# Second mixer: per-image products as 32x32 tiles of TensorE, layer norms applied by ScalarE, row loop written out

## The reference, cut to what matters

```python
x = x + _L1_conv_ref(_ln_c(x), ...)            # _ln_c: layer norm over the 96 channels, eps 1e-6

zxbcdt = xf @ W_in                             # z (192), xBC (224), dt (12)
dt = softplus(dt + dt_bias)
xBC = silu(conv3x3_depthwise(xBC) + b_conv)    # x_inner 192, B_state 16, C_state 16
Y_diag = einsum('bclhn,bcshn,bhcls,bcshp->bclhp', Cm, Bm, L, X)
states = einsum('bclhn,bhcl,bclhp->bchpn', Bm, decay_states, X)
Y_off  = einsum('bclhn,bchpn,bhcl->bclhp', Cm, states, state_decay_out)
y = Y_diag + Y_off + x_inner * D_param
y = layernorm(y, eps=1e-5) * gamma + beta      # over 192
y = (y * silu(z)) @ W_out
```

## Time and profile before

| | |
|---|---|
| median of 3 runs | 2666.05 us (2660.29 to 2674.77) |
| profiled execution | 2666.47 us, its span 2664.7 us |
| busy in the span: TensorE, VectorE, ScalarE, GpSimd | 1986.0, 1728.5, 1063.6, 1371.1 us |
| second mixer, 970 to 1945 us: the same | 881.66, 804.24, 363.21, 493.51 us |
[...]

### The profile page before, as it was taken

The page is one execution under the profiler, slowest core; times in us unless marked ns, Lnnn a source line. Parts: engine busy times, 40 slices in busy tenths (PEclk is TensorE's granted clock), DMA queues, the critical chain, the costliest instruction groups (busy, mean ns, idle before and its releaser), DMA issues.

```text
span 2664.7 us, 63187 instructions
## 1 busy us (share of the span) xinstructions
PE 1986.0 (75%) x24050; PEld 1660.2 (62%) x24050; DVE 1728.5 (65%) x5157; ACT 1063.6 (40%) x1936; POOL 1371.1 (51%) x1285
## 2 busy tenths in 40 slices
PE   3666433249999938999899989999975331699997
PEld 2555433237777727888788778888864331477775
DVE  4778644325766647888888878888856432366665
ACT  2233111037777723433333434333311110477775
POOL 2111155546877725555545545555533555477776
PEclk8667555569999968989998988899865555799999
DMA  7100011156666550000000000000000113466654
GB/s 140 39 21 21 6 50 51 65 207 208 203 208 207 166 95 2 3 3 3 3 3 2 3 3 3 2 3 2 3 2 18 52 53 124 138 210 206 205 194 126
DMA packets 99374, 203.29 MB, mean 76 GB/s; under 512 B 53158, under 2 KB 58911, under 8 KB 99096
## 3 DMA queue, kind: packets, MB, share of 16 engines
q10 hardware_dynamic: 21312, 102.00, 11.5%
q1 hardware_dynamic: 56024, 59.20, 8.3%
q0 software_dynamic: 21760, 38.33, 4.1%
HBM read 148.85 MB, written 52.58 MB: 76 GB/s over the span
## 4 chain that ended last, share of the span: by engine, by line
PE 26%; issue 14%; POOL 10%; DVE 8%; another core or an unknown queue 4%; DMA 1%; ACT 1%; SPq 0%; POOLq 0%; ACTq 0%; DVEq 0%
PE ps L938 4%; PE ps L939 4%; PE ps L940 4%; PE ps L1048 3%; POOL arena L663 3%; POOL w L644 2%; PE ps L1089 2%; PE ps L1109 2%; PE ps L970 2%; PE ps L1076 1%; POOL xn L655 1%; POOL arena L669 1%; PE ps L1093 1%; DVE arena L1159 1%
## 5 line engine op out<-in xcount | busy, mean ns | idle before, releaser
L1048 PE MATMUL ps<-rounded 128*128 128x224 f32 (+1 forms) x2256 | 373.3, 310 | 41.3 <-ACT rounded L801 18.2
L938 PE MATMUL ps<-rounded 97*128 97x512 f32 (+2 forms) x952 | 391.3, 411 | 9.2 <-issue 3.0
L1048 PEld LDWEIGHTS ps<-rounded 128*128 128x128 f32 x2256 | 325.7, 211 | 86.5 <-issue 33.9
L939 PE MATMUL ps<-rounded 97*128 97x512 f32 (+2 forms) x952 | 377.3, 396 | 0.0
L940 PE MATMUL ps<-rounded 97*128 97x512 f32 (+2 forms) x952 | 376.6, 396 | 0.0
L566 POOL DMA_INDIRECT rows<-arena x256 | 246.7, 964 | 216.2 <-DVEq L1453 140.6
L1520 DVE TENSOR_TENSOR rounded<-arena,rounded 128x512 fp32r<-128x512 f32 x296 | 225.4, 762 | 199.9 <-ACT arena L780 167.7
L779 ACT ACTIVATE rounded<-ps 128x512 fp32r<-128x512 f32 x444 | 267.5, 602 | 169.8 <-PE ps L940 138.5
L598 POOL TENSOR_TENSOR rounded<-arena,rounded 128x512 fp32r<-128x512 f32 x148 | 192.8, 1303 | 169.3 <-DVE arena L1503 94.1
L780 ACT ACTIVATE arena<-ps 128x512 f32<-128x512 f32 x444 | 267.1, 601 | 0.0
L970 PE MATMUL ps<-gw,arena 97*128 97x4 f32 x512 | 113.5, 347 | 172.6 <-issue 98.6
(11 more groups left out here) (229 smaller groups left out, 4358.5 us busy)
## 6 DMA issues: line engine op xcount, KB each, us to landing
rounded<-weights_by_expert ACTq DMA_DIRECT2D x148, 673.0 KB
arena<-rows SPq DMA_DIRECT2D x74, 392.0 KB
rows<-xn SPq DMA_DIRECT2D x17, 392.0 KB
residual<-in_x SPq DMA_DIRECT2D x16, 384.0 KB, 6.2
residual<-after_ffn SPq DMA_DIRECT2D x16, 384.0 KB, 6.0
weights_by_expert<-rounded SPq DMA_DIRECT2D x8, 672.0 KB, 3.2
rows<-arena POOLq DMA_INDIRECT x256
after_ffn<-arena POOLq DMA_INDIRECT x148
```

What stands on the lines that cost most here:

```text
L938: pe.matmul(dst, left[0], right[0], start=start, stop=False)
L939: pe.matmul(dst, left[1], right[0], start=False, stop=False)
L1048: pe.matmul(dst[:, 0:w], x3[:, x_part, n, slot, tokens], wtap[:, w_part, n, y + 1, 0:w], start=(y == 0 and n == x_part == w_part == 0), st ...
```

## The change

It has four parts. The three products over B and C (lines 1085, 1093, 1073) take the transposed rows (or the rows) directly, as four products of one image each, which sit in four different 32x32 tiles of the array; `images_apart` and its buffers go. The two layer norms of the mixer are applied on ScalarE as `Identity(scale * x + bias)`, four instructions for a quad; GpSimd makes the bias with a second small operation, and VectorE keeps the statistics. The loop of 32 steps is written out, so that all 152 steps are straight code. A few waits go with it: PE waits on the transposes themselves, VectorE's `gather` and `norm_y` wait until ScalarE has used the buffers of the quad before.

```diff
+        def signed_stats(dve, ch, src, n, width, which_eps, own):
...
+            ch.done(dve.tensor_scalar(mo[:, 0, :], mo[:, 0, :], -0.5, None, ALU.mult))
...
+        def scale_and_bias(pool, ch, n, count, own):
+            _, mom, has_var, has_rstd = own
+            pool.wait_ge(has_var, count)
+            ch.link(pool.tensor_tensor(mom[:, 5, 0:n], mom[:, 4, 0:n], half_neg[:, 0:n], ALU.pow))
+            pool.tensor_tensor(mom[:, 1, 0:n], mom[:, 0, 0:n], mom[:, 5, 0:n], ALU.mult).then_inc(has_rstd, 1)
...
-            with eng.Fori(0, G - 1) as g:
...
+            for r in range(-HEAD, SIDE * G + TAIL):
...
-                    images_apart(g, c)
                     steps_from(g, c, 0)
...
+            def apply_norm(dst, src, own, has_rstd, count, done):
+                act.wait_ge(has_rstd, count)
+                for n in range(Q):
+                    ins = act.activation(dst(n), src(n), ACT.Identity, bias=own[:, 1, n:n + 1], scale=own[:, 5, n:n + 1])
+                ins.then_inc(done, 1)
+
             def step(g, r):
                 if (i := row(g, r, 0)) is not None:
                     conv_tanh(g, i)
+                if (c := quad(g, r, 10)) is not None:
+                    apply_norm(lambda n: u4[:, n, :], lambda n: yy[:, c % 2, n, :], moments_y, s["rstd_y"], c + 1, s["u"])
+                if (k := quad(g, r, -5)) is not None:
+                    rows_of = xr[:, k // NQ, k % NQ * Q:(k % NQ + 1) * Q, :]
+                    apply_norm(lambda n: xn[:, k % 2 * Q + n, :], lambda n: rows_of[:, n, :], moments, rstd_ready, LN_MIX1 + k + 1, s["ln"])
                 if (k := quad(g, r, 1 - T_AHEAD)) is not None:
                     shift_rest(g, k)
...
-                pe.matmul(bank(4)[:, NH * SIDE:NH * SIDE + SIDE], b_apart[:, c % 2, i % Q, :], ct[:, c % 2, i % Q, :], start=True, stop=True)
+                for pb in images:
+                    of = slice(pb.start, pb.start + NS)
+                    pe.matmul(bank(4)[pb, NH * SIDE:NH * SIDE + SIDE], bt[of, c % 2, i % Q, :], ct[of, c % 2, i % Q, :], start=True, stop=True)
...
-                pe.matmul(bank(5)[:, INNER:2 * INNER], c_apart[:, c % 2, j, :], st[:, :, :].rearrange("p a b -> p (a b)"), start=True, stop=True)
+                for pb in images:
+                    of = slice(pb.start, pb.start + NS)
+                    pe.matmul(bank(5)[pb, INNER:2 * INNER], ct[of, c % 2, j, :], st[of, :, :].rearrange("p a b -> p (a b)"), start=True, stop=True)
...
-                pe.matmul(bank(6)[:, 0:INNER], b_rows[:, c % 2, j, :], xw[:, c % 2, j, :, :].rearrange("p a b -> p (a b)"), start=True, stop=True).then_inc(s["ds_pe"], 1)
+                for pb in images:
+                    ins = pe.matmul(bank(6)[pb, 0:INNER], xbc[pb, c % 2, j, INNER:CONV], xw[pb, c % 2, j, :, :].rearrange("p a b -> p (a b)"), start=True, stop=True)
+                ins.then_inc(s["ds_pe"], 1)
...
+                if j == 0:
+                    need(dve, s["u"], c - 1)
...
-                if (c := quad(g, r, 10)) is not None:
-                    norm_y(g, c, 1)
-                if (k := quad(g, r, -5)) is not None:
-                    norm_x(g, k, 1)
```

More of the change, by code:

```diff
@@ L270, in metaformer @@
         wdt = part(Q, NH)
-        bt = part(Q, SIDE)
+        bt = part(2, Q, SIDE)
         ct = part(2, Q, SIDE)
-        b_apart = part(2, Q, P)
         xdt = part(2, Q, NH, HD)
@@ L347, in metaformer @@
         y_norm = (stats_y, moments_y, s["var_y"], s["rstd_y"])
+        def signed_stats(dve, ch, src, n, width, which_eps, own):
+            sums, mom, has_var, _ = own
+            for r in range(n):
+                ch.done(dve.bn_stats(sums[:, r, :], src(r)))
+            ch.wait()
+            sv, mo = sums[:, 0:n, :], mom[:, :, 0:n]
+            ch.done(dve.tensor_tensor(mo[:, 0, :], sv[:, :, 1], sv[:, :, 4], ALU.add))
+            ch.done(dve.tensor_tensor(mo[:, 1, :], sv[:, :, 1], sv[:, :, 4], ALU.subtract))
+            ch.link(dve.tensor_tensor(mo[:, 2, :], sv[:, :, 2], sv[:, :, 5], ALU.add))
+            ch.done(dve.tensor_scalar(mo[:, 0, :], mo[:, 0, :], -0.5, None, ALU.mult))
+            ch.link(dve.tensor_tensor(mo[:, 1, :], mo[:, 1, :], mo[:, 1, :], ALU.mult))
+            ch.link(dve.scalar_tensor_tensor(mo[:, 3, :], mo[:, 1, :], width / 4.0, mo[:, 2, :], ALU.mult, ALU.add))
+            dve.tensor_scalar(mo[:, 4, :], mo[:, 3, :], 1.0 / width, which_eps, ALU.mult, ALU.add).then_inc(has_var, 1)
+        def scale_and_bias(pool, ch, n, count, own):
[3 more added lines that the diff above has]
+            pool.tensor_tensor(mom[:, 1, 0:n], mom[:, 0, 0:n], mom[:, 5, 0:n], ALU.mult).then_inc(has_rstd, 1)
         def row_stats(dve, ch, src, n, width, which_eps, own):
@@ L371, in metaformer, with steps_of_rows @@
         LN_MIX1 = G
-        def steps_of_rows(eng, step, enter=None, leave=None, weights=None):
-            for r in range(-HEAD, TAIL):
+        def steps_of_rows(step, weights=None):
+            for r in range(-HEAD, SIDE * G + TAIL):
                 if r == 0 and weights:
                     weights()
-                step(0, r)
-            with eng.Fori(0, G - 1) as g:
[L382 to L388, removed]
                 step(0, r)
@@ L646, in steps_from @@
                     tri.unsqueeze(1).to_broadcast([P, NH, SIDE]), ALU.mult).then_inc(s["r"], 1)
[L648 to L659, removed]
             def scaled(c, dst, by, done):
@@ L687, in step @@
                 if (c := quad(g, r, 9)) is not None:
-                    rstd(pool, Q, g * NQ + (c + 1), y_norm)
+                    scale_and_bias(pool, ch, Q, c + 1, y_norm)
                 if (k := quad(g, r, -6)) is not None:
-                    rstd(pool, Q, g * NQ + (LN_MIX1 + k + 1))
-            steps_of_rows(pool, step)
+                    scale_and_bias(pool, ch, Q, LN_MIX1 + k + 1, token_norm)
+            steps_of_rows(step)
             route(1)
@@ L863, in step @@
                     act.activation(sp[:, 1, :], sp[:, 0, :], ACT.Exp, scale=-1.0).then_inc(s["exp_dt"], 1)
-            steps_of_rows(act, step)
+            steps_of_rows(step)
             act.wait_ge(stage_end, 3)
@@ L1065, in sums @@
                 ins.then_inc(s["cs"], 1)
+            images = [slice(b * SIDE, (b + 1) * SIDE) for b in range(PACK)]
             def pairs(g, i):
@@ L1132, in step @@
                     pairs(g, i)
-            steps_of_rows(pe, step, weights=lambda: pe.wait_ge(prep_done, 2))
+            steps_of_rows(step, lambda: pe.wait_ge(prep_done, 2))
             pe.wait_ge(stage_end, 3)
@@ L1186, in time_steps_begin @@
                 dve.wait_ge(s["cv_ev"], g * SIDE + (Q * q + Q))
-                ch.done(dve.transpose(bt[:, :, :], xbc[:, q % 2, :, INNER:INNER + SIDE]))
+                ch.done(dve.transpose(bt[:, q % 2, :, :], xbc[:, q % 2, :, INNER:INNER + SIDE]))
                 dve.transpose(ct[:, q % 2, :, :], xbc[:, q % 2, :, INNER + NS:INNER + NS + SIDE]).then_inc(s["bt"], 1)
@@ L1228, in add_output, with norm_y, norm_x @@
                 dve.tensor_tensor(rows, rows, bank(3)[:, 0:Q * D].rearrange("p (a b) -> p a b", b=D), ALU.add).then_inc(s["o_add"], 1)
[L1230 to L1236, removed]
+            def norm_y(g, c):
+                ch.wait()
+                need(dve, s["u"], c)
+                signed_stats(dve, ch, lambda n: yy[:, c % 2, n, :], Q, INNER, 1e-5, y_norm)
+            def norm_x(g, k):
+                if k % NQ == 0:
+                    dve.wait_ge(x_in, 64 * (G + k // NQ + 1))
+                need(dve, s["ln"], k)
+                signed_stats(dve, ch, lambda n: quad_rows(g, k)[:, n, :], Q, D, 1e-6, token_norm)
             def step(g, r):
@@ L1296, in weights @@
                 dve.memset(st[:, :, :], 0.0).then_inc(s["state"], 1)
[L1298 to L1302, removed]
+            steps_of_rows(step, weights)
             dve.wait_ge(s["o_add"], G * NQ)
```

14 lines of the change are left out of this document (4 added, 10 removed).

## The result

The changed kernel takes 2766.72 us (median of 4 runs, 2755.84 to 2773.43) against 2666.54 us before on the same chip: ratio 1.037, 95% interval 1.0326 to 1.0414. It is slower by 100 us; the forecast was slower, 2817 us, with a range of 2655 to 2920.

The account below looks back on a forecast made before the run. TensorE was taken to set the pace, with ScalarE's chain to `shift_rest` pacing full-clock quads. Norms +132, clock +31, tiles -6, back edges -6 make +151 us on 2666.5: 2817 us, range 2655 to 2920.

Parts of the forecast that it names:

- The bound: Second mixer: TensorE sets the pace, but ScalarE's chain to `shift_rest` already paces quads whenever TensorE runs at full clock.
- The norm of y: On ScalarE ahead of `shift_rest`: delays it 3.7 us, paid fully at full clock, 2.3 us at half clock.
- The norm of the input: On ScalarE ahead of `affine`: TensorE's second `u_columns` gets 2.3 us of new wait, bounds 1.3 to 2.6.
- S: Start of TensorE's convolution in the quad step with the norm of the input; that norm's times count from it.
- Norms and clock: Second mixer, 31 quads: the two norms add 132 us and the lower TensorE clock 31 us.
- What VectorE saves: Work taken off VectorE gains nothing: it turns into idle time, and the 1.64 us wait for `attend` stays.
- Rival 1: Second mixer: relief of VectorE and GpSimd ends the wait for `attend`; faster, 2600 or 2520 us; chance 0.15.
- Two such edges: -6 us: Loop of steps: writing it out removes two back edges costing TensorE 2.96 us each, -6 us.
- "-6 us" for the tiles: TensorE's scan: four-tile products save perhaps 0.1 us a step in about half of 128 steps, -6 us.
- `images_apart` goes; no engine was waiting for it, so 0: GpSimd: removing its `images_apart` operations changes the time by 0, since no engine waited for them.
- Rival 3: TensorE's tiled products run one after another, some 2.9 us more in a step; 3050 us; chance 0.04.
- The clock: TensorE: more idle time drops it to half clock in more quads, 1 us each (bounds 0 and 3), +31 us.

Follow-up runs that it names:

- e4: Changed kernel with both norms still on ScalarE but at the end of its step, behind `shift_rest` and both `affine`; ratio 0.983 to the kernel before.
- e12: Changed kernel with the norm of y on VectorE and the norm of the input on ScalarE behind both `affine`; ratio 0.981 to the kernel before.
- e9: Changed kernel with the four activations of the norm of y made twice, the first into unread memory; ratio 1.062 to the kernel before.
- e1: Changed kernel with both norms back on VectorE, tiles and written-out loop kept; ratio 0.982 to the kernel before, mixer 925.1 us.
- e6: Kernel before with only the loop written out; norms on VectorE, whole-array products; ratio 0.991 to the kernel before, mixer 942.7 us.
- e5: Changed kernel with the three products back on the whole array and `images_apart` on GpSimd; ratio 1.040 to the kernel before, mixer 1064.8 us.
- e10: As e1, with GpSimd still making its three spreading operations per quad into unread memory; ratio 0.989 to the kernel before, mixer 950.4 us.
- e11: As e1, with three unread TensorE products per quad in the wait for `attend`; ratio 0.974 to the kernel before, mixer 898.0 us.
- e8: Changed kernel with five unread TensorE products per quad ahead of the wait for `shift_rest`; ratio 1.039 to the kernel before, mixer 1064.1 us.
- e7: Changed kernel with only the norm of the input back on VectorE, the norm of y still on ScalarE; ratio 1.033 to the kernel before.
- e1 again: The kernel e1 run once more, as base on the same chip as later variants; ratio 0.984 to the kernel before, mixer 927.4 us.

## Why the prediction was right, and where it was off

**The bound.** That ScalarE's chain to `shift_rest`, with ScalarE busy 37% of the stage before, would pace the quads was right; the place in the queue (e4, e12) and the doubled norm (e9) show it. One reading was off: the four waits at the weight load stand at convolutions for which TensorE waits too, so it was 12 quads of 32 that waited, not 16. With 12 quads at 6.0 us and 19 at 2.5 the prediction's own sum for the norms would have been 120, not 132.

**The norm of y.** Predicted 3.7 us, 3.5 measured in the quad shown. GpSimd's second operation took 0.20 us (0.25 taken). The activation took 0.536 us on average over the stage (0.535 taken), so the 186 ns for scale and bias, the prediction's pointer cost, holds. But four of them took 1.86 us, not 2.2: added up they are 2.14, so each of the three that follow another overlaps it by 0.09 us. The prediction had them one behind another, as the casts of `shift_rest` are: 1.02 and three times 0.60 us, in 2.86 us. The groups of the changed kernel:

```profile
L833 ACT ACTIVATE arena<-arena,moments_y 128x192 f32<-128x192 f32 x120 | 55.8, 536 | 51.8 <-POOL moments_y L361 51.8
L833 ACT ACTIVATE xn<-residual,moments 128x96 f32<-128x96 f32 x120 | 46.2, 456 | 11.4 <-POOL moments L361 10.7
```

**The norm of the input.** Its scale and bias were ready at S + 4.31 (4.3 predicted). TensorE got to its second `u_columns` at S + 7.6 instead of S + 4.65, 2.95 us later; predicted were 2.3 of wait and 1 for the clock. The split was different: in this quad the convolution ran at a clock of 0.50 (1360.50 to 1365.30), `conv_tanh` ended at S + 5.2, so the norm waited for it and not for GpSimd, and only 0.65 us of wait was left. Over the stage the wait for `affine` was 0.9 us in 24 quads, 21.5 us in all.

**Both together.** Norms and clock were 132 + 31 = 163 us in the sum; taking them away gave 151. That these are so near is in part luck: against e1 TensorE is idle 102 us longer, where the terms of the norms had 132, and busy 49 us longer, where the clock had 31.

**What VectorE saves, and the wait for `attend`.** Right in the main: with 109 us less work on VectorE, the wait is still 1.45 us instead of 1.64. Rival 1 is out.

**The steps that were mis-sized.** The forecast of 2817 was for the profiled execution, which took 2773.4, 44 us less; in the mixer it was 151 predicted and 110 measured. The mechanism was right, and sizes were off. "Two such edges: -6 us": the written-out loop alone was worth 24 us. For the rest the size depends on the order in which the parts are added, since they act on each other:

| order, in us of the mixer | loop | tiles, no `images_apart` | norms and clock | sum |
|---|---|---|---|---|
| predicted | -6 | -6 | +163 | +151 |
| loop, tiles (e6, e1), norms | -24 | -18 | +151 | +110 |
| loop, norms (e6, e5), tiles | -24 | +11 | +122 | +110 |

That each measured row adds to some 110 is no evidence: the steps run from the kernel before to the changed one. The +11 may be chance; by the whole executions the last row is -24, +1 and +124, with a sum of 100. With VectorE applying the norms, the terms that failed are "-6 us" for the tiles and "`images_apart` goes; no engine was waiting for it, so 0": together they were worth 18 us. With the operations of `images_apart` put back (e10) all of that was gone, and VectorE's product beside them took 1.76 us instead of 0.68. With the norms on ScalarE they were worth nothing (e5), and it is the norms' 163 that was too large. That the tiles brought TensorE itself a gain is not seen: with GpSimd's operations put back, e10 is no faster than the whole-array kernel e6 (950.4 and 942.7 us). A single scan is shorter: ahead of `u_columns`, as in rows 8, it takes 1.61 us in the tiled kernel e11 (1301.49 to 1303.10) against 1.77, which bears out the 0.1 us of the prediction. The stage as a whole does not show it.

**Rival 3.** Its 3050 us does not follow from its terms: 2.9 us in half of the 128 steps would be 186 on top of 2817, that is 3003, and in all of them 3188. Both are far from what was measured.

**The clock.** It fell as predicted, from 0.89 to 0.85. In the changed kernel giving it back brought nothing that can be measured (e8); where TensorE is the bound, it was worth 29 us (e11). With the norm of y alone on ScalarE it fell furthest, to 0.81, and there no filled variant was run.

**What stays open.** How the loop's 24 us divide between its edges, the clock and the rest; how much the filling in e8 took back; how much of e7's loss is the lower clock itself; and why norms and tiles act on each other as the table shows.

## What to carry to other kernels

Before moving work to an engine with a low busy share, look at what stands behind it in that engine's queue and who waits for that: here the same eight activations cost 151 us at the head of ScalarE's step and nothing at its end. An operation that nobody waits for was not free here: beside GpSimd's three spreading operations a product of VectorE took 1.76 us instead of 0.68, and the mixer was 23 us longer (e10). Compare the duration of the same instruction with and without its neighbour. And where TensorE was the bound and had a short wait in each quad, three small products into a bank that is overwritten anyway raised its mean clock from 0.91 to 0.97 and took 29 us of 927 off the mixer (e11). Where ScalarE was the bound, five of them raised it from 0.85 to 0.91 and brought nothing that can be measured (e8).

## What the runs showed of the hardware that I had not expected

- VectorE's 96x512 product in `gate` took 0.68 us without GpSimd's spreading operations and 1.76 us with them (e1 again, e10).
- Four activations with scale and bias from SBUF, 0.536 us each, took 1.86 us back to back in the changed kernel, 0.28 us less than their sum. Four casts of line 801, 1.02 and three times 0.60 us, took 2.86 us in the kernel before, with no overlap.
- Three unread products in each quad's wait for `attend` raised TensorE's mean clock over the stage from 0.91 to 0.97 (e1 again, e11).
- The kernel before took 2556 us on one chip and 2661 to 2670 us on others, a difference of 4%. The kernel e1 took 2507.8 us on one and 2623.5 us on another, while its mixer was 925.1 and 927.4 us: the difference lies in the other stages.
